# Expert rows padded to 64 instead of 128 in a one-core decoder layer: 32 whole and 4 split tiles in place of 39

## The chip, the cores and the metric

The kernel runs on one core of a Trainium2 chip. The metric is the device time of one execution in microseconds (us); lower is better. The reference's outputs are float32; most matmuls work on pairs of float16 parts (a high part and the remainder), three products for each product of the reference.

## The reference, cut to what matters

One decoder layer on x of shape (8, 256, 256): causal self-attention with 16 heads, a cross-attention of three iterations with a GRU, and a feed-forward with a shared expert and 8 routed experts, of which each token takes two. After each of the three there is a residual and a layer norm. The change touches only the third:

```python
router_probs = softmax(einsum('bsd,de->bse', x, gate_w) + gate_b)
expert_values, expert_indices = top_k(router_probs, k=2)
expert_values = expert_values / (sum(expert_values, axis=-1, keepdims=True) + 1e-09)
h = gelu(einsum('bsd,edi->bsei', x, ew1) + eb1)
all_outputs = einsum('bsei,eid->bsed', h, ew2) + eb2
moe_out = einsum('bse,bsed->bsd', weights_E, all_outputs)
return x + _mlp(x, sh_w1, sh_b1, sh_w2, sh_b2) + moe_out
```

There are T = 2048 tokens, D = 256, I = 1024, E = 8 experts. The kernel computes only the two chosen experts of each token, so 4096 (token, expert) rows.

## The kernel before, in words

**Stages.** Attention takes about the first 0.4 of the span, the cross-attention runs to about 585 us, the shared expert and the routing to about 647 us, the routed experts to about 877 us, and the combine with the last norm to the end. All five engines run programs written out by hand; every dependence is a semaphore.

**Shared expert and routing (about 585 to 647 us).** `ffn_tensor` runs 24 of 32 steps m of the shared expert: `up(m)` is six matmuls of 512 columns, `down(m - 2)` twelve of 256. Between them, listed in `beside`, are the small matmuls of the routing. `ffn_vector` runs `choose_experts`, `count_tokens`, `weigh_choices`, `place_rows`, `part_choices`, `name_rows` and `name_tiles`: some fifty small VectorE operations that depend on one another through the semaphore `r_line`. They count the rows of each expert, give each expert a whole number of 128-row tiles (`tiles`, `ends`, `first`), and give each row its slot. `rows_of(n)` on TensorE (L1955, in steps 16 to 19) turns slots into token numbers; it waits for `part_choices(n)` (L2113, L2117, L2120). The results are `dst` (128 x NTILE, the token row of each place of each tile, or a dummy row for an empty place) and `tile_e` (the expert of each tile). The constant TILES_KNOWN is the value of `r_line` when `tile_e` is ready. GpSimd subtracts the float16 part of each hidden chunk (`hidden_low`, L1839) and issues the gathers.

**Tiles.** NTILE = 2T/128 + E - 1 = 39 tiles of 128 rows. This is the number that always suffices, whatever the router chooses. For every tile i, with double buffers u = i % 2:

1. GpSimd gathers 128 token rows of `rows_x` into `xg` (`gather`, L1769), in its loop in `experts_pool`.
2. TensorE transposes them (`turn`, L1875, two float32 transposes), ScalarE and VectorE split them into `xgT` (L2348, L2392).
3. Up (L2257): for each of 8 chunks k of the hidden dimension, six matmuls of 128 columns. The expert's weight `e1[:, e, ch, h, k]` is the stationary side, `xgT` streams. Three products for each of two halves of D; the weight part h = 0 is used twice in a row, h = 1 once, so there are four different weights for a chunk. The expert number is a register value, so the weight's address is worked out on TensorE's sequencer.
4. VectorE adds the bias (`biased`, L2408), ScalarE applies gelu and casts (`front`, L2354, L2360), VectorE takes the remainder (`hidden_low`, L2413): the hidden parts `he`.
5. Down (L2265, L2266): for each k, `he[u][0][:, k]` is the stationary side and both parts of `e2[:, e, k]` stream (512 columns), then `he[u][1][:, k]` with 256 columns. The stationary side has a fixed address, the streamed one is worked out at run time. The tile's rows come out as PSUM partitions.
6. VectorE adds both halves and the bias (`back`, L2424, L2427) into `yo`, ScalarE scales each row by its router weight (`weigh`, L2366), and GpSimd adds it to `back_y` in DRAM by an indirect DMA (`scatter`, L2229). Each scatter waits for the one before to have landed.

**Order.** TensorE's pass i is `turn(i + 3)`, then `tile_pair(i + 2, .., i, ..)`: the up of tile i + 2 with the down of tile i, interleaved three up matmuls to one down matmul. The first two ups run alone; the last two downs run alone too, each behind one `up(MF + ..)` of the rest of the shared expert. After them come steps MF + 2 to MS of the shared expert, `add_sums` (L2306) and `last_downs`. Expert numbers are loaded into registers 16 at a time (`experts_from`), in passes 14 and 30. ScalarE's pass is `turned(i + 3)`, `weigh(i - 1)`, `front(i + 2)`; `front(i)` waits, before its cast L2360, for D_mm of tile i - 2. VectorE's is `turned(i + 3)`, `biased(i + 2)`, `back(i)`, `hidden_low(i + 2)`.

**Combine.** SyncE waits for all scatters, then loads `back_y` in 8 chunks (`combine_load`, L2463). VectorE takes the statistics (L2494), GpSimd the reciprocal roots, ScalarE and VectorE normalise, SyncE stores (L2476).

Of the kernel before, what the change touches and what calls it, by code (L numbers as in the profile page):

```python
# [34 lines left out]
def decoder_layer(nc, a, out):  # L35
# [17 lines left out]
    NTILE = 2 * T // P + E - 1  # L53
# [3 lines left out]
    with top:  # L57
# [17 lines left out]
        dst = sb(top, "dst", [P, NTILE], I32)  # L75
# [13 lines left out]
        ramp_i = sb(top, "ramp_i", [P, NTILE], I32)  # L89
# [17 lines left out]
        tile_e = sb(top, "tile_e", [P, NTILE], I32)  # L107
# [8 lines left out]
        def constants_pool():  # L116
# [14 lines left out]
            PO.iota(ramp_i[:, :], pattern=[[1, NTILE]], base=0, channel_multiplier=0).then_inc(const_fill, 1)  # L131
# [944 lines left out]
        n_back, n_sum, n_stat, n_rstd, n_norm = (sem(k) for k in ("n_back", "n_sum", "n_stat", "n_rstd", "n_norm"))  # L1076
        NSTAT = 2 * TG + 1
# [6 lines left out]
        NUMBERED = 46  # L1084
# [16 lines left out]
        def norm_sum(g):  # L1101
# [3 lines left out]
                             rows, ALU.add).then_inc(n_sum, 1)  # L1105
            VE.wait_ge(n_sum, g + 1)
            for t in range(TG):
                VE.bn_stats(st2[g % 2][:, t, :], xs[:, g * TG + t, :]).then_inc(n_stat, 1)
            VE.wait_ge(n_stat, NSTAT * g + TG)
# [4 lines left out]
            VE.wait_ge(n_stat, NSTAT * g + 2 * TG)  # L1114
# [567 lines left out]
        with ExitStack() as c:  # L1682
# [22 lines left out]
            def route(*shape):  # L1705
# [13 lines left out]
            cmp1, up8 = route(E, NT), route(E, E)  # L1719
            s1, s2, m2, p2, r0, r1 = (route(NT) for _ in range(6))  # L1720
            slot, top_w = route(2, NT), route(NT, 2)
            total, tiles, ends, first = (route(E) for _ in range(4))
            te_f, ramp, cnt = route(NTILE), route(NTILE), route(1)
            HALF = NT // 2
            behind, places, turn_at = route(1), route(P), route(NT)
# [4 lines left out]
            ramps = reused[:, 0:P + 2 * NT + 1].bitcast(I32)  # L1730
            meant = part(reused, 0, HALF * NTILE, F16).rearrange("p (t n) -> p t n", n=NTILE)
            cmp2 = reused[:, 0:NTILE * E].rearrange("p (t e) -> p t e", e=E)
# [7 lines left out]
            picked = mask[:, 5 * NTILE:6 * NTILE]  # L1740
            ROUND = 1.5 * 2.0 ** 23
# [13 lines left out]
                sem(k) for k in ("U_mm", "U_bias", "U_gelu", "U_hi", "U_lo", "D_mm", "D_out"))  # L1755
            gathered = [sem(f"gathered{q}") for q in range(NT // 2)]
# [7 lines left out]
            NAMED, TILES_KNOWN = NUMBERED + 6, NUMBERED + 11  # L1764
# [53 lines left out]
            def number_constants():  # L1818
# [4 lines left out]
                    (0, NT), (NT, P), (NT + P, NT), (2 * NT + P, 1)))  # L1823
                PO.iota(turns, pattern=[[P, NT]], base=0, channel_multiplier=0).then_inc(made, 1)
# [193 lines left out]
            PARTED = 34  # L2018

            def choose_experts():  # L2020

# [197 lines left out]
            def experts_pool():  # L2219


                def scatter(i):
# [4 lines left out]
                    if i >= 1:  # L2227
                        PO.wait_ge(rows_out[(i - 1) % 2], 16 * ((i - 1) // 2 + 1))
# [347 lines left out]
```

## Time and profile before

| what | us |
|---|---|
| time of the kernel, median of 3 runs | 908.75 |
| lowest of the 3 runs | 908.33 |
| highest of the 3 runs | 1269.37 |
| span of the profiled execution, first to last instruction | 905.5 |
| TensorE busy in the span | 876.6 (97%) |
| VectorE busy | 648.3 (72%) |
| ScalarE busy | 557.3 (62%) |
| GpSimd busy | 365.5 (40%) |

For the profiled execution itself only the span is given, no device time of its own beside it. The 1269.37 us run is an outlier; the two others agree within 0.05%. PE is TensorE's matmuls, PEld its weight loads (they overlap), DVE is VectorE, ACT ScalarE, POOL GpSimd, SP SyncE. Ends of matmuls are modelled, so starts are what to read. L12 is line 12 of the kernel.

### The profile page before, as it was taken

What the parts mean: (1) busy time and instruction counts of PE and PEld (TensorE: products, weight loads), DVE (VectorE), ACT (ScalarE), POOL (GpSimd) and SP (SyncE); (2) the same over time, 40 slices, a digit from 0 to 9 for tenths busy, and PEclk for the clock granted to TensorE, in tenths of its full rate; (3) what the DMA queues carried; (4) which work ended last, traced back from release to release, by engine and by line L of the source; (5) the groups of instructions that cost most, each with busy time, mean ns of one, the idle gap of its engine ahead of it and who ended that gap; (6) DMA issues with size and microseconds to landing.
All of it is one profiled execution on the core that took longest, in us unless ns stands there. A gap on an engine that the chain in (4) does not pass through costs nothing. (4 is left out here: it accounts for less than half of the span.)

```text
span 905.5 us, 23841 instructions
## 1 busy us (share of the span) xinstructions
PE 876.6 (97%) x8190; PEld 669.9 (74%) x8190; DVE 648.3 (72%) x1839; ACT 557.3 (62%) x1347; POOL 365.5 (40%) x492
## 2 busy tenths in 40 slices
PE   5999999999999999999999999999999999999996
PEld 4777777777777777776767676676788888888864
DVE  5667787867676777667878786869677766776655
ACT  6778776767666677656575755545455555554555
POOL 2333433333333465325444442354534444444433
PEclk9999999999999999999999999999999999999998
DMA  9742434242423241230000000099443332333226
GB/s 320 195 141 96 163 107 151 94 142 93 140 76 125 95 150 49 9 94 2 1 1 2 1 1 1 32 356 409 135 107 49 49 49 44 49 49 48 43 30 192
DMA packets 61584, 88.09 MB, mean 97 GB/s; under 512 B 17279, under 2 KB 46527, under 8 KB 61343
## 3 DMA queue, kind: packets, MB, share of 16 engines
q1 hardware_dynamic: 53439, 75.52, 25.3%
q0 software_dynamic: 7488, 10.27, 7.3%
q8 instruction: 72, 1.18, 0.6%
q10 hardware_dynamic: 544, 0.79, 0.3%
q14 instruction: 41, 0.34, 0.1%
HBM read 56.00 MB, written 30.56 MB: 96 GB/s over the span
## 5 line engine op out<-in xcount | busy, mean ns | idle before, releaser
L2257 PE MATMUL ps<-slots,e 128*128 128x128 f16 x1872 | 189.9, 219 | 2.2 <-DVE xs L2424 2.2
L669 POOL TENSOR_SCALAR prob<-prob,rden 128x128 f32<-128x128 f32 (+1 forms) x256 | 110.7, 448 | 200.9 <-DVE rden L958 200.9
L2257 PEld LDWEIGHTS ps<-slots,e 128*128 x1872 | 152.4, 97 | 35.4 <-issue 5.1
L855 ACT ACTIVATE prob<-prob,nmx 128x128 f32<-128x128 f32 (+1 forms) x256 | 114.1, 450 | 40.8 <-DVE nmx L951 37.9
L2265 PE MATMUL ps<-e,xT 128*128 x312 | 117.3, 378 | 0.0
L2354 ACT ACTIVATE slots<-slots 128x512 f32<-128x512 f32 x78 | 49.2, 631 | 107.0 <-DVE slots L2408 107.0
L31 PE MATMUL ps<-xT,wqkv 128*128 128x256 f16 x768 | 96.1, 275 | 0.4 <-DVE wqkv L938 0.4
L31 PEld LDWEIGHTS ps<-xT,wqkv 128*128 128x128 f16 x768 | 70.4, 98 | 29.6 <-issue 21.7
L2266 PE MATMUL ps<-e,xT 128*128 x312 | 85.1, 273 | 0.0
L1769 POOL DMA_INDIRECT xg<-rows_x,dst x39 | 40.9, 1049 | 106.5 <-DVE mask L2397 103.2
L951 DVE CUSTOM_DVE_ANT_0 prob<-ps,mask 128x128 f32<-128x128 f32 (+1 forms) x256 | 75.9, 353 | 3.9 <-PE ps L749 3.9
L2413 DVE TENSOR_TENSOR xT<-slots,xT 128x1024 f16<-128x1024 f32 x39 | 47.8, 1225 | 39.9 <-ACT xT L2360 39.9
L2229 POOL DMA_INDIRECT back_y<-xs,dst x39 | 62.6, 1606 | 29.0 <-DMA back_y<-xs,dst 12.2
L2408 DVE SCALAR_TENSOR_TENSOR slots<-ps,b1e 128x512 f32<-128x512 f32 x78 | 53.8, 692 | 26.5 <-PE ps L2257 26.3
L965 DVE COPY pT<-ps 128x384 f32<-128x384 f32 x64 | 35.6, 556 | 40.8 <-PE ps L720 40.5
L971 DVE TENSOR_TENSOR oT<-ps,oT 128x256 f16<-128x256 f32 x64 | 27.2, 425 | 46.4 <-ACT oT L879 45.9
L749 PE MATMUL ps<-qk 64*128 64x128 f32 (+1 forms) x512 | 59.3, 350 | 0.7 <-ACT qk L865 0.7
L31 PE MATMUL ps<-an,wqkv 120*128 120x256 f16 x432 | 59.0, 272 | 1.0 <-POOL an L1502 1.0
L614 DVE SCALAR_TENSOR_TENSOR parted<-piece,parted 128x256 f16<-128x256 f32 x144 | 57.1, 421 | 0.0
L759 PE MATMUL ps<-pT,v 128*64 128x128 f32 x768 | 56.1, 281 | 0.7 <-DVE pT L965 0.7
L872 ACT COPY pT<-ps 128x384 f32<-128x384 f32 x64 | 30.6, 478 | 41.5 <-PE ps L720 40.1
L720 PE MATMUL ps<-ident,prob 128*128 128x128 f32 x384 | 52.7, 273 | 2.4 <-DVE oT L971 2.0
(275 smaller groups left out, 1939.0 us busy)
## 6 DMA issues: line engine op xcount, KB each, us to landing
halves<-parted SPq DMA_DIRECT2D x36, 512.0 KB, 2.9
piece<-in_L_ffn_ew SPq DMA_DIRECT2D x32, 512.0 KB, 4.5
e<-halves SPq DMA_DIRECT2D x16, 1024.0 KB, 15.4
piece<-in_L_ffn_sh_w SPq DMA_DIRECT2D x4, 512.0 KB, 9.4
sw<-halves SPq DMA_DIRECT2D x4, 512.0 KB, 6.3
rows_x<-xs SPq DMA_DIRECT2D x4, 512.0 KB, 7.7
xs<-back_y SPq DMA_DIRECT2D x8, 256.0 KB, 5.0
out<-xs SPq DMA_DIRECT2D x8, 256.0 KB, 2.1
```

The source lines that it names most:

```text
L31: mm = pe.matmul(out, w, x, start=first and n == 0, stop=last and n == len(products) - 1, **kw)
L614: VE.scalar_tensor_tensor(share(piece_part(q, 1)), share(like_part(q)), WS, share(piece_part(q, 0)), ALU.mult, ALU.subtract).then_inc(p_lo, 1)
L669: PO.tensor_scalar(prob[m % 3][:, h, r], prob[m % 3][:, h, r], rden[m % 2][:, h, t:t + 1], 1.0, ALU.mult, ALU.mult).then_inc(normed, 1)
L749: mm = PE.matmul(ps[:, 2 + h, query_tile(t)], qk[m % 2][r, 0, t * P:t * P + P], qk[m % 2][r, 1, 0:(t + 1) * P], start=True, stop=True)
L759: mm = PE.matmul(ps[r, 4 + t, 384:512], v_sb[m // 2 % 2][:, key, m % 2, r], pT[:, h, at:at + P], start=key == 0, stop=key == t, skip_group ...
L855: SC.activation(p, p, ACT.Exp, bias=nmx[u][:, h, t:t + 1], scale=-1.0, accum_out=den[u][:, h, t:t + 1]).then_inc(exped, 1)
L951: VE.tensor_tensor_reduce(prob[m % 3][:, h, r], ps[:, 2 + h, r], mask[:, r], -1.0, HIGHEST, ALU.add, ALU.min, nmx[m % 2][:, h, t:t + 1]).t ...
L2229: PO.indirect_dma_start(back_y, bass.IndirectOffsetOnAxis(ap=dst[:, i:i + 1], axis=0), yo[i % 2], None, compute_op=ALU.add).then_inc(rows_ ...
L2257: yield PE.matmul(ps[:, 2 * u + q, (k % 4) * P:(k % 4) * P + P], w[ch][h], xgT[u][j][:, ch, :], start=n == 0, stop=n == 3 * DC - 1)
L2265: yield PE.matmul(ps[:, 4 + u, :], he[u][0][:, k, :], w, start=k == 0, stop=False, skip_group_check=True)
L2266: yield PE.matmul(ps[:, 4 + u, 0:D], he[u][1][:, k, :], w[:, 0:D], start=False, stop=k == IC - 1, skip_group_check=True)
L2408: VE.scalar_tensor_tensor(z, ps[:, 2 * u + q, :].rearrange("p (k t) -> p k t", k=4), 1 / WS, bias, ALU.mult, ALU.add).then_inc(U_bias, 1)
```

## The change

Each expert gets a whole number of 64-row halves instead of 128-row tiles. An expert with an odd number of halves has a single half left over; at most 8 experts do, and two such halves share a split tile. So 32 whole tiles (FULL) and 4 split tiles suffice always. `tile_e` has 40 names: one for each whole tile, two for each split one.

- `place_rows` counts whole tiles and single halves apart (`parts`, 256 comparisons in place of 128), works out `paired` and `onward`, and moves the rows of single halves: seven more VectorE operations and several longer ones. `name_tiles` has five more. `name_halves`, new, makes two lists for the scatters of each split tile: rows of the other half point to the dummy rows. It stands after the second tile in VectorE's program.
- Up of a split tile: for each chunk and each of the two experts six matmuls of 64 columns.
- Down of a split tile (`split_down`): the weight is now the stationary side and the hidden half streams with 64 columns, so the result comes out transposed. VectorE copies it (`split_out`), TensorE turns it back (`split_back`, two float32 transposes), VectorE adds the bias for each half (`split_rows`).
- Order: whole tiles go on in pairs (passes 0 to 29); the ups of tiles 32 and 33 go beside the downs of 30 and 31; from pass 32 on, nothing is interleaved.
- A split tile is scattered twice, the second after the first has landed.
- The sum count `n_sum` is folded into `n_stat`, with no change of order.

The core of the diff:

```diff
-    NTILE = 2 * T // P + E - 1
+    HALF_P = P // 2
+    FULL = 2 * T // P
+    NTILE = FULL + E // 2
+    NAMES = FULL + 2 * (NTILE - FULL)
...
 place_rows:
-                VE.tensor_tensor(cmp1, ps[:, 7, E:2 * E].unsqueeze(2).broadcast_to((P, E, NT)), ...
+                VE.tensor_tensor(cmp1, ps[:, 7, E:2 * E].unsqueeze(2).broadcast_to((P, E, 2 * NT)), ...
+                VE.tensor_tensor(parts[:, 0, :], parts[:, 0, :], parts[:, 1, :], ALU.subtract)
+                VE.tensor_scalar(paired, parts[:, 1, :], float(P), None, ALU.mult)
+                VE.tensor_tensor(w0, rank, paired.unsqueeze(1).broadcast_to((P, NT, E)), ALU.is_ge)
+                VE.tensor_scalar(onward, ends[:, 1, :], -float(P), float(HALF_P * (UNITS - 1)), ALU.mult, ALU.add)
+                VE.scalar_tensor_tensor(onward, first[:, 0, :], -float(HALF_P), onward, ALU.mult, ALU.add)
+                VE.tensor_tensor(w0, w0, onward.unsqueeze(1).broadcast_to((P, NT, E)), ALU.mult)
+                VE.tensor_tensor(bf, bf, w0, ALU.add)
...
 scatter:
+                    for m in range(2):
+                        at = NTILE + 2 * (i - FULL) + m
+                        if m == 1:
+                            PO.wait_ge(rows_out[i % 2], rows_gone(i) - 16)
+                        PO.indirect_dma_start(back_y, bass.IndirectOffsetOnAxis(ap=dst[:, at:at + 1], axis=0),
+                                              yo[i % 2], None, compute_op=ALU.add).then_inc(rows_out[i % 2], 16)
...
+                def up_chunk(i, experts, k):
+                    u, q, wide = i % 2, k // 4, P // len(experts)
+                    for m, e in enumerate(experts):
+                        w = [[e1[:, bass.ds(e, 1), ch, h, k * P:k * P + P].squeeze(1) for h in range(2)]
+                             for ch in range(DC)]
+                        at = k % 4 * P + m * wide
+                        for n, (ch, (h, j)) in enumerate(itertools.product(range(DC), HILO)):
+                            yield PE.matmul(ps[:, 2 * u + q, at:at + wide], w[ch][h],
+                                            xgT[u][j][:, ch, m * wide:(m + 1) * wide], start=n == 0, stop=n == 3 * DC - 1)
...
+                def split_down(i, experts):
+                    u = i % 2
+                    by_half = e2[:, :, :, :, :].rearrange("p e (a b) i n -> p (e a) b i n", a=2)
+                    down_ready(i)
+                    for k in range(IC):
+                        for c, (m, e) in itertools.product(range(DC), enumerate(experts)):
+                            rows, at = slice(m * HALF_P, (m + 1) * HALF_P), c * P + m * HALF_P
+                            w = [by_half[:, bass.ds(e * 2 + k // 4, 1), k % 4, h, c * P:c * P + P].squeeze(1) for h in range(2)]
+                            for n, (h, j) in enumerate(HILO):
+                                mm = PE.matmul(ps[:, 4 + u, at:at + HALF_P], w[h], he[u][j][:, k, rows],
+                                               start=k == 0 and at == 0 and n == 0, stop=k == IC - 1 and n == 2,
+                                               skip_group_check=True)
+                    mm.then_inc(D_mm, 1)
...
 TensorE, pass i:
+                    if i < FULL:
+                        tile_pair(i + 2, i, names)
                     else:
-                        up(MF + i - (NTILE - 2))
-                        tile_pair(None, None, i, expert[i])
+                        if i + 2 < NTILE:
+                            tile_up(i + 2, names)
+                        else:
+                            up(MF + i - (NTILE - 2))
+                        if i > FULL:
+                            split_back(i - 1)
+                        split_down(i, experts_of(names, i))
                 for m in range(MF + 2, MS):
                     up(m)
+                    if m == MF + 2:
+                        split_back(NTILE - 1)
...
 ScalarE, pass i:
-                    if i >= 1:
+                    if 1 <= i <= FULL:
                         weigh(i - 1)
                     if i + 2 < NTILE:
                         front(i + 2)
                     else:
                         hidden(MF + i - (NTILE - 2))
-                weigh(NTILE - 1)
+                    if i > FULL:
+                        weigh(i - 1)
                 for m in range(MF + 2, MS):
                     hidden(m)
+                    if m == MF + 2:
+                        weigh(NTILE - 1)
...
 VectorE, pass i:
+                    if i < FULL:
+                        back(i, names[i])
+                    if i > FULL:
+                        split_rows(i - 1, experts_of(names, i - 1))
+                    if i >= FULL:
+                        split_out(i)
                     if i + 2 < NTILE:
                         hidden_low(i + 2)
```

## Rows read from the trace of the kernel before

**Rows 1.** The page: parts 1 and 5 (busy us, mean ns | idle before)

```profile
PE 876.6 (97%) x8190; PEld 669.9 (74%) x8190; DVE 648.3 (72%) x1839; ACT 557.3 (62%) x1347; POOL 365.5 (40%) x492
...
L2257 PE MATMUL ps<-slots,e 128*128 128x128 f16 x1872 | 189.9, 219 | 2.2 <-DVE xs L2424 2.2
```

**Rows 2.** Windows: 676 to 856 us; PE, PEld, DVE, ACT, POOL, clock, DMA, GB/s

```profile
676.00:856.00 180.00, 177.81 (x2079) 150.25 (x2077) 124.15 (x252) 94.91 (x159) 80.90 (x63) 1.00 0.31 49
```

**Rows 3.** Timeline of PE: the transposes of tiles 7 and 38

```profile
680.75 0.38 PE L1875 MATMUL ps<-ident,xg 128*128 128x128 f32 x2
...
858.28 0.38 PE L1875 MATMUL ps<-ident,xg 128*128 128x128 f32 x2
```

**Rows 4.** The chain that ended last: the lone up of tile 1

```profile
654.14 4.03 PE ps L2257 x48
```

**Rows 5.** Lines L2257 and L2265: register operations on TensorE's sequencer (ns min/median/max)

```profile
L2257 PEldq FUSED_REGOPS  x1248: 46/46/46, 648.7 to 869.0; - x179
...
L2265 PEldq ALU_OP  x312: 32/32/42, 658.7 to 874.3; - x156
```

**Rows 6.** Timeline of PE: shared ups around the lone downs

```profile
869.52 1.46 PE L31 MATMUL ps<-xT,sw 128*128 128x512 f16 x6
...
877.31 1.46 PE L31 MATMUL ps<-xT,sw 128*128 128x512 f16 x6
```

**Rows 7.** Timeline: weight loads of the first rows_of (39 columns each)

```profile
625.96 0.27 PEld L1955 LDWEIGHTS ps<-slots 128*128 128x128 f16 x8 [1.21 <-DVE slots L2120]
```

**Rows 8.** Timeline from the last scatters to the last matmuls

```profile
877.75 1.55 POOL L2229 DMA_INDIRECT back_y<-xs,dst  x1 [2.92 <-DMA back_y<-xs,dst]
...
882.30 1.55 POOL L2229 DMA_INDIRECT back_y<-xs,dst  x1 [3.00 <-DMA back_y<-xs,dst]
...
885.96 3.99 SPq L2463 DMA_DIRECT2D xs<-back_y  x8
...
891.63 1.90 PE L2306 MATMUL ps<-xs,routes 128*128 128x256 f32 x8
...
893.37 4.09 PE L31 MATMUL ps<-sw,slots 128*128 128x256 f16 x36
...
898.37 0.76 DVE L2494 BATCH_NORM_STATS2 routes<-ps 128x6 f32<-128x256 f32 x2
```

**Rows 9.** Windows: the clock (1.00 is 2.4 GHz) in two stretches

```profile
901.00:903.00 2.00, 0.00 (x0) 0.00 (x0) 1.26 (x3) 0.78 (x2) 0.00 (x0) 0.50 0.77 258
654.00:658.00 4.00, 4.00 (x50) 3.24 (x47) 2.38 (x5) 1.79 (x3) 0.26 (x1) 1.00 0.72 238
```

**Rows 10.** Timeline of PE at the kernel's start: the same matmuls twice

```profile
10.49 2.62 PE L31 MATMUL ps<-xT,wqkv 128*128 128x256 f16 x12 [0.43 <-DVE wqkv L938]
...
14.72 1.49 PE L31 MATMUL ps<-xT,wqkv 128*128 128x256 f16 x12
```

**Rows 11.** Timeline of the routing, 617 to 647 us

```profile
617.78 0.29 DVE L2078 TENSOR_REDUCE routes<-routes 128x8 f32<-128x128 f32 x1
...
618.62 1.09 DVE L2085 TENSOR_TENSOR routes<-routes 128x8 f32<-128x8 f32 x1
...
625.97 0.37 PE L1955 MATMUL ps<-slots 128*128 128x39 f16 x8 [0.72 <-DVE slots L2120]
...
638.85 0.18 DVE L2150 CAST tile_e<-routes 128x39 int32<-128x39 f32 x1
...
646.93 0.38 PE L1875 MATMUL ps<-ident,xg 128*128 128x128 f32 x2
```

**Rows 12.** Timeline: VectorE's part of turned(3) and TensorE's turn(4)

```profile
662.72 0.42 DVE L2392 TENSOR_TENSOR slots<-ps,slots 128x256 f16<-128x256 f32 x1
...
663.88 0.38 PE L1875 MATMUL ps<-ident,xg 128*128 128x128 f32 x2
```

**Rows 13.** Groups of instructions by line, 676 to 856 us: cast and scale

```profile
L2360 ACT CAST xT<-slots 128x1024 f16<-128x1024 f32 x32 | 33.5, 1045 | 1.0
...
L2366 ACT ACTIVATE xs<-xs,mask 128x256 f32<-128x256 f32 x32 | 16.3, 509 | 0.0
```

More of the change, by code:

```diff
@@ L1740, in decoder_layer @@
             picked = mask[:, 5 * NTILE:6 * NTILE]
+            apart, own = mask[:, 6 * NTILE:7 * NTILE - FULL], mask[:, 7 * NTILE:7 * NTILE + 1]
+            sides = [mask[:, 7 * NTILE + 1 + m:7 * NTILE + 2 + m] for m in range(2)]
+            split_to = mask[:, 8 * NTILE:8 * NTILE + NAMES - FULL].rearrange("p (t m) -> p t m", m=2)
             ROUND = 1.5 * 2.0 ** 23
@@ L2294, in tile_pair @@
                                 last_down = mm
-                        if up is not None and k % 4 == 3:
+                        if k % 4 == 3:
                             last_up.then_inc(U_mm, 1)
-                    if down is not None:
-                        last_down.then_inc(D_mm, 1)
+                    last_down.then_inc(D_mm, 1)
                 def add_sums():
@@ L2407, in biased @@
                             VE.wait_ge(U_lo, i)
-                        VE.scalar_tensor_tensor(z, ps[:, 2 * u + q, :].rearrange("p (k t) -> p k t", k=4), 1 / WS,
-                                                bias, ALU.mult, ALU.add).then_inc(U_bias, 1)
+                        for m, e in enumerate(experts):
+                            rows = slice(m * wide, (m + 1) * wide)
+                            bias = b1e[:, bass.ds(e, 1), 4 * q:4 * q + 4].squeeze(1).unsqueeze(2).broadcast_to((P, 4, wide))
+                            done = VE.scalar_tensor_tensor(z[:, :, rows], up[:, :, rows], 1 / WS, bias, ALU.mult, ALU.add)
+                        done.then_inc(U_bias, 1)
                 def hidden_low(i):
@@ L2428, in back, with split_out, split_rows @@
                                             ALU.add).then_inc(D_out, 1)
+                def split_out(i):
+                    VE.wait_ge(D_mm, i + 1)
+                    if i >= FULL + 2:
+                        VE.wait_ge(Y_mm, i - FULL - 1)
+                    VE.tensor_copy(yT[:, i % 2, :], ps[:, 4 + i % 2, 0:D]).then_inc(D_out, 1)
+                def split_rows(i, experts):
+                    u = i % 2
+                    VE.wait_ge(Y_mm, i - FULL + 1)
+                    VE.wait_ge(rows_out[u], rows_gone(i - 2))
+                    for m, e in enumerate(experts):
+                        rows = slice(m * HALF_P, (m + 1) * HALF_P)
+                        done = VE.scalar_tensor_tensor(yo[u][rows, :], ps[rows, 4 + u, D:2 * D], 1 / WS,
+                                                       b2e[rows, bass.ds(e, 1), :].squeeze(1), ALU.mult, ALU.add)
+                    done.then_inc(D_out, 1)
                 VE.wait_ge(r_line, TILES_KNOWN)
-                expert = experts_from(mybir.EngineType.DVE, 0)
+                names = experts_from(mybir.EngineType.DVE, 0)
                 turned(0)
@@ L2435, in experts_vector @@
                 for i in range(2):
-                    biased(i, expert[i])
+                    biased(i, names)
                     hidden_low(i)
@@ L2440, in experts_vector @@
                         shared_base(2)
+                name_halves()
                 for i in range(NTILE):
-                    if (i + 2) % LOADED == 0 and i + 2 < NTILE:
-                        expert += experts_from(mybir.EngineType.DVE, i + 2)
+                    if (i + 2) % LOADED == 0 and i + 2 < NAMES:
+                        names += experts_from(mybir.EngineType.DVE, i + 2)
                     if i + 3 < NTILE:
```

240 lines of the change are left out of this document (156 added, 84 removed).

## The prediction

> **What bounds the kernel now.** The page comes first. TensorE is busy 97% of the span, no other engine over 72%, and the costliest group is L2257, the experts' up projections with 1,872 matmuls [rows 1]. Next the windows: between 676 and 856 us TensorE is busy 177.81 of 180 us, VectorE 124, ScalarE 95, GpSimd 81, at granted clock 1.00 [rows 2]. So in the loop over expert tiles the time of a tile is TensorE's. The timeline gives it: the transposes (L1875) that open a pass start at 680.75 and, 31 passes later, at 858.28 [rows 3], 5.73 us each. Two of the 31 passes load expert names into registers and take about 1.2 us more; the others take 5.65 us.
>
> What fills 5.65 us? The transposes take 0.38 [rows 3]. The rest is 48 up matmuls of 128 columns, 8 down matmuls of 512 and 8 of 256: 12,288 columns in some 5.27 us, 0.43 ns a column, which is the 2.4 GHz level. A paired pass is bound by columns. But the first up projection runs alone, and there 48 matmuls (6,144 columns) take 4.03 us [rows 4], 84 ns each and not the 55 of their columns. Every expert weight has an address made at run time: TensorE's sequencer issued 1,248 FUSED_REGOPS of 46 ns for L2257 and 312 ALU_OPs of 32 ns for L2265 [rows 5]: 32 and 8 per tile. 4.03 us over 32 addresses is 126 ns per address, each with its loads and the one or two matmuls that use it. So there are two bounds: columns (0.43 ns each) and weight addresses (126 ns each). A paired pass needs 32 x 0.126 = 4.03 us plus 8 ALU_OPs for addresses, below 5.27, and the wide down matmuls hide them. That margin is what the change uses up.
>
> **The change, part by part.** All sums are against the span of 905.5 us; the median of the timed runs, 908.75, is 3.25 us above it, and I add that at the end.
>
> *What goes.* 39 tiles become 36. Paired passes of two whole tiles fall from 37 to 30: 7 x 5.65 = 39.6 us. The two passes that hold a down projection alone (869.52 to 877.31, 3.9 us each, of which 1.3 is a shared up of six 512-column matmuls [rows 6]) lose 2 x 2.6 = 5.2 us. Together 44.8.
>
> *A split up projection.* Its matmuls have 64 columns, twice as many, for two experts: 64 addresses instead of 32. The columns would cost 6,144 x 0.43 = 2.6 us, the addresses 64 x 0.126 = 8.06 us. The trace has no 64-column matmul with a run-time address. The bounds are 27 ns for each of the 96 (64 columns; the loads of eight matmuls of 39 columns at fixed addresses took 0.27 us [rows 7], and with 0.10 for the last the other seven are (0.27 - 0.10)/7 = 25 ns apart) and 84 ns (the lone up, with the same form of address and also two addresses to three matmuls [rows 4]). I take 84 ns: the split only doubles the number of such groups. Tiles 32 and 33 go up beside whole downs (which add 8 ALU_OPs, between 0 and 0.15 us each, since (5.27 - 4.03)/8 = 0.15; I take 0.11): 8.06 + 0.9 + 0.38 = 9.35 us, twice, 18.7. Tiles 34 and 35 go up alone: 8.06 + 0.38 and 8.06, 16.5.
>
> *A split down projection.* It no longer streams the weight (512 columns, one ALU_OP for two matmuls); it loads it as the stationary side: 8 chunks x 2 column halves x 2 experts x 2 parts = 64 addresses. Its index is `e * 2 + k // 4`, one or two register operations more; going from an ALU_OP of one to a FUSED_REGOPS (46 against 32 ns, [rows 5]) an operation costs little, say 7 ns. Bounds: 2.6 us (columns) to 10.9 us (the extra ones as an instruction of their own, 170 ns per address); I take 64 x 0.134 = 8.6 us. Four of them, none beside anything: 34.4. Three transposes back inside the loop: 3 x 0.4 = 1.2.
>
> Loop: 18.7 + 16.5 + 34.4 + 1.2 - 44.8 = +26.0 us, for three tiles fewer.
>
> *The scatters.* Each split tile adds to back_y twice, the second waiting for the first to land. Before, where one scatter waits for the last, they start 4.55 us apart (877.75, 882.30) and the last lands at 885.96, 3.66 us on, when the loads of the combine start [rows 8]. In the whole tiles this has room (one per 5.65). Now look at ScalarE's program order: `weigh(i - 1)` stands behind `front(i + 2)` for split tiles, and `front(35)` waits for D_mm of tile 33. So tile 32 is scaled only after the down of tile 33 ends; call that T. Then come the cast (1.05) and the scale (0.5) [rows 13]: the first of eight half scatters starts at T + 1.7 and the eighth lands at T + 1.7 + 7 x 4.55 + 3.66 = T + 37.2. TensorE's last two passes take 2 x (1.3 + 0.4 + 8.6) = 20.6, so the loads of the combine start 16.6 us after the last down, where before it was 8.5 (877.47 to 885.96). Tail: +8.1 us. The shared ups and downs that follow (877.5 to 891.6, some 14 us [rows 6, 8]) no longer cover it: the first chunk landed about 5.2 us after its load began (885.96, VectorE and TensorE go on at 891.2 and 891.63), so TensorE idles about 16.6 + 5.2 - 14.7 = 7 us before `add_sums` (L2306 [rows 8]).
>
> *The clock.* Before, TensorE's last matmuls end at 897.46 [rows 8], and over 901 to 903 the granted clock is 0.50, its 1.2 GHz level [rows 9]. So after 7 us idle add_sums and the first of the last downs start at that level: 1.74 us (891.63 to 893.37) becomes 3.5, and at the kernel's start 12 matmuls of 256 columns took 2.62 us, and 1.49 a little later [rows 10]. Some 2.9 us more (1.74 and, for 12 matmuls, 1.13), 0.9 of it covered (the last downs end at 897.46, VectorE takes their sums at 898.37 [rows 8]): +2.0.
>
> *The head.* place_rows runs on VectorE while TensorE waits: its first routing matmul (L1955, 625.97) sits idle 0.72 us for L2120 [rows 11], so what is added there is added to the end. Seven more small operations (128 elements 0.29 us [rows 11], 8 or 16 elements about 0.17, and 0.03 between), 1.7 us, and longer ones (256 for 128 elements, a ramp of 116 for 39), 0.5: +2.2. It can be 1 us more where one is held up, as L2085 was (8 elements, 1.09 us [rows 11]). name_tiles' added 1.6 us cost nothing: the names are known at 639.0, and TensorE loads them one shared pass (some 2.6 us) before turn(0) at 646.93 [rows 11], near 644. name_halves (7 operations, 1.3 us) stands on VectorE ahead of turned(3), done at 663.14 while TensorE wants it at 663.88 [rows 12]: 1.3 - 0.7 = +0.7 (0 to 1.5). VectorE's split halves of the bias and of the output, and the iotas, lie beside a TensorE that is now slower: nothing.
>
> Sum: +26.0 + 8.1 + 2.0 + 2.2 + 0.7 = +39.0. Span 944.5; with 3.25, 947.8 us.
>
> **Rivals.**
> *A, columns set the split tiles.* If half-width matmuls cost their columns and the address work is hidden, a split tile costs 2.6 up and 2.6 down. For it: the 39-column loads [rows 7] and the paired passes. Against: [rows 4], a lone up at 84 ns with column time of 55. To T the time from pass 30 is then 2 x 5.65 + 3.0 + 2.6 + 2.6 + 0.4 + 2.6 = 22.5 us, plus 37.2 for the scatters, 59.7; before it is 7 x 5.65 + 7.8 + 8.5 = 55.9. So +3.9, head 2.9, clock 2.0: 917.5, not slower by the measure used here. It decides if an address costs under about 60 ns. The Trainium skill, "TensorE: Matmul & The Clock Gate", section "Back-to-back issue gap", gives this price: a warm matmul's gap is its columns over 2.4 GHz plus 2.5 ns, never under about 25 ns. The same section has 81 ns for a stream of loads and matmuls at 128 columns, near the 84 here, but without the address operations.
> *B, the added index operations are instructions of their own*: 10.9 us a down, of which two lie before T and the last two are hidden by the scatters: +4.6, 952.
> *C, half scatters are cheaper or overlap* (only 64 rows carry values). For it: the 3.66 us of landing is most of the 4.55. Against: each still moves 128 rows. Then the tail is about +3 and the clock does not fall: 941.
> *D, the clock falls in the split passes*, with their narrow matmuls. At 1.2 GHz the mixed passes are bound by columns again (10.6 us, +1.3 each), and the shared matmuls behind double and outlast the scatters: +10, 958. Against: over the lone up, 654 to 658, the granted clock stayed at 1.00 [rows 9].
>
> **How the numbers follow.** Forecast 0.52, A 0.10, B 0.13, C 0.17, D 0.08. The time is the forecast's, 947. The range 928 to 960 leaves out A and a little above D. A measurement of this kernel tells about 2% (18 us) from no change: slower by more, over 927, holds the forecast, B, C and D, 0.88; within it A and a small remainder, 0.10; faster by over 2% would need a scatter chain that vanishes too, 0.02.
>
> **What would show it.** In the profile after: the paired whole passes unchanged at 5.65 us; about 16 us between the starts of the last lone passes; FUSED_REGOPS of 64 per split up and 64 per split down, and split matmuls 80 to 90 ns apart; eight scatters about 4.5 us apart after the down of tile 33, the loads of the combine waiting for the last, and TensorE idle before add_sums at clock 0.5; the first L1955 waiting near 3 us. Split matmuls under 40 ns apart would prove the forecast wrong (A); scatters under 3 us apart would prove its tail wrong.

## The result and the profile after

| | before | after |
|---|---|---|
| median of the timed runs, us | 908.76 | 944.07 |
| span of the profiled execution, us | 905.5 | 941.0 |
| TensorE busy in the span, us | 876.6 | 906.5 |
| mean granted clock | 0.997 | 0.973 |

The change makes the kernel slower: the ratio of the times is 1.0403, with an interval of 1.0389 to 1.0417. The forecast was 947.8 us by the sum (stated as 947), in a range of 928 to 960. The page of the kernel after, parts 1, 2 (the clock) and 5, answers to [rows 1]:

```profile
PE 906.5 (96%) x8512; PEld 694.3 (74%) x8512; DVE 642.3 (68%) x1846; ACT 548.7 (58%) x1332; POOL 364.6 (39%) x493
...
PEclk9999999999999999999999999999999999996578
...
L2343 PE MATMUL ps<-slots,e 128*128 128x128 f16 (+1 forms) x1920 | 189.1, 218 | 2.1 <-DVE xs L2560 1.1
```

TensorE is busy 30 us longer although three tiles are gone, and its clock falls late in the span. L2343 is now the up, L2351 and L2352 the whole tiles' down, L2366 the split down, L1904 the transposes that open a pass, L2375 the transposes back. The timeline of TensorE, from the pass with tile 30's down on, answers to [rows 3] and [rows 6]:

```profile
831.12 0.38 PE L1904 MATMUL ps<-ident,xg 128*128 128x128 f32 x2
...
841.55 0.39 PE L1904 MATMUL ps<-ident,xg 128*128 128x128 f32 x2
...
851.51 0.40 PE L1904 MATMUL ps<-ident,xg 128*128 128x128 f32 x2
...
877.29 0.67 PE L2375 MATMUL ps<-ident,routes 128*128 128x128 f32 x2
877.75 8.35 PE L2366 MATMUL ps<-xT,e 128*128 128x64 f16 x96
886.10 2.72 PE L31 MATMUL ps<-xT,sw 128*128 128x512 f16 x6
888.61 0.63 PE L2375 MATMUL ps<-ident,routes 128*128 128x128 f32 x2
```

The two mixed passes (a split up beside a whole down) take 10.43 and 9.96 us. From 851.5 to 886.1 there are two split ups and two split downs, 8.4 to 8.6 us each. The chain that ended last shows all four; these are its rows for the first up and the first down (start, us, what; a "PE" piece counts its matmuls):

```profile
851.90 3.71 PE ps L2343 x45
855.71 4.59 PE ps L2343 x51
860.31 3.93 PE ps L2366 x45
864.30 4.62 PE ps L2366 x51
```

96 matmuls in 8.6 us are 90 ns each. The register operations by line, answering to [rows 5], give what they wait for. 1,280 for the ups are 32 for each of 32 whole tiles and 64 for each of 4 split ones; the 256 of the split downs are 64 each:

```profile
L2343 PEldq FUSED_REGOPS  x1280: 46/46/46, 650.4 to 877.1; - x183
...
L2366 PEldq FUSED_REGOPS  x256: 46/46/60, 860.2 to 905.7; - x128
```

The scatters and the loads of the combine, from the timeline (first, second and last of eight half scatters), answer to [rows 8]:

```profile
887.92 2.00 POOL L2312 DMA_INDIRECT back_y<-xs,dst  x1 [31.03 <-ACT xs L2495]
...
892.59 1.55 POOL L2312 DMA_INDIRECT back_y<-xs,dst  x1 [2.67 <-DMA back_y<-xs,dst]
...
918.32 1.55 POOL L2312 DMA_INDIRECT back_y<-xs,dst  x1 [2.49 <-DMA back_y<-xs,dst]
...
922.25 3.95 SPq L2624 DMA_DIRECT2D xs<-back_y  x8
...
927.76 3.36 PE L2428 MATMUL ps<-xs,routes 128*128 128x256 f32 x8 [5.13 <-DMA xs<-back_y]
```

GpSimd (POOL) had waited 31 us for ScalarE's scaling and starts 1.8 us after the down of tile 33 has ended at 886.10. Then each scatter waits for the one before, on average 4.34 us from start to start, and TensorE idles 5.13 us. The head, answering to [rows 11]: the first routing matmul waits 3.06 us where it had waited 0.72.

```profile
628.06 0.37 PE L1984 MATMUL ps<-slots 128*128 128x36 f16 x8 [3.06 <-DVE slots L2164]
```

The span is 35.5 us longer. In three stretches: up to the transposes of tile 33, which stood at 828.86 and stand at 831.12, +2.26; from there to the loads of the combine, 57.10 us before (to 885.96) and 91.13 after (to 922.25), +34.03; from the loads to the end, 19.54 before and 18.75 after, -0.79.

### The profile page after: what moved, and what is told of

It is laid out like the page before. It is cut to its first block and busy times, and to the rows that moved or that the text cites. A ratio compares the mean times of both kernels' runs of the same rounds, so it can differ in the third digit from the quotient of the medians.

```text
span 941.0 us, 24674 instructions
## 1 busy us (share of the span) xinstructions
PE 906.5 (96%) x8512; PEld 694.3 (74%) x8512; DVE 642.3 (68%) x1846; ACT 548.7 (58%) x1332; POOL 364.6 (39%) x493
## 5 line engine op out<-in xcount | busy, mean ns | idle before, releaser
L2343 PE MATMUL ps<-slots,e 128*128 128x128 f16 (+1 forms) x1920 | 189.1, 218 | 2.1 <-DVE xs L2560 1.1
L2343 PEld LDWEIGHTS ps<-slots,e 128*128 x1920 | 152.7, 98 | 35.7 <-issue 5.1
L2483 ACT ACTIVATE slots<-slots 128x512 f32<-128x512 f32 x72 | 45.3, 630 | 115.9 <-DVE slots L2544 110.6
L2351 PE MATMUL ps<-e,xT 128*128 x256 | 96.8, 378 | 0.1
L31 PEld LDWEIGHTS ps<-xT,wqkv 128*128 128x128 f16 x768 | 70.4, 98 | 29.6 <-issue 21.8
L2544 DVE SCALAR_TENSOR_TENSOR slots<-ps,b1e 128x512 f32<-128x512 f32 (+1 forms) x80 | 50.0, 636 | 39.7 <-PE ps L2343 39.4
L1788 POOL DMA_INDIRECT xg<-rows_x,dst x36 | 37.1, 1032 | 97.3 <-DVE mask L2529 81.1
L2352 PE MATMUL ps<-e,xT 128*128 x256 | 69.8, 273 | 0.0
L2549 DVE TENSOR_TENSOR xT<-slots,xT 128x1024 f16<-128x1024 f32 x36 | 44.1, 1225 | 36.4 <-ACT xT L2489 36.4
L975 DVE COPY pT<-ps 128x384 f32<-128x384 f32 x64 | 35.5, 555 | 40.9 <-PE ps L730 40.6
L2303 POOL DMA_INDIRECT back_y<-xs,dst x32 | 51.1, 1598 | 24.1 <-ACT xs L2495 14.6
L2016 ACT ACTIVATE slots<-ps,b1s 128x512 f32<-128x512 f32 x32 | 22.0, 687 | 57.6 <-PE ps L31 47.5
```

Of the source, the lines that this page charges most:

```text
L31: mm = pe.matmul(out, w, x, start=first and n == 0, stop=last and n == len(products) - 1, **kw)
L2303: PO.indirect_dma_start(back_y, bass.IndirectOffsetOnAxis(ap=dst[:, i:i + 1], axis=0), yo[i % 2], None, compute_op=ALU.add).then_inc(rows_ ...
L2343: yield PE.matmul(ps[:, 2 * u + q, at:at + wide], w[ch][h], xgT[u][j][:, ch, m * wide:(m + 1) * wide], start=n == 0, stop=n == 3 * DC - 1)
L2351: yield PE.matmul(ps[:, 4 + u, :], he[u][0][:, k, :], w, start=k == 0, stop=False, skip_group_check=True)
L2352: yield PE.matmul(ps[:, 4 + u, 0:D], he[u][1][:, k, :], w[:, 0:D], start=False, stop=k == IC - 1, skip_group_check=True)
```

## The experiments

**Is it the addresses?** The first run takes the address work away and leaves every matmul; it leaves out the right choice of experts in the split tiles.

```diff
-                        w = [[e1[:, bass.ds(e, 1), ch, h, ...
+                        w = [[e1[:, (bass.ds(e, 1) if wide == P else slice(m, m + 1)), ch, h, ...
-  w = [by_half[:, bass.ds(e * 2 + k // 4, 1), k % 4, h, ...
+  w = [by_half[:, 2 * m + k // 4, k % 4, h, ...
```

> The changed kernel, with the expert weights of the four split tiles taken at fixed addresses (experts 0 and 1) instead of addresses worked out at run time; the split tiles so compute with the wrong experts, everything else is as in the changed kernel. Theory 1 (the price of a split tile is its 64 + 64 run-time weight addresses): no register operations are left between the split matmuls, they start 27 to 30 ns apart, a lone split up or down takes 2.6 to 2.9 us instead of 8.6, the two mixed passes fall from about 10.2 to 5.7 us, the clock stays at 1.00, and, the eight scatters after the down of tile 33 being as they were, the time falls by some 32 us to about 912. Rival (the price lies in the 64-column matmuls and their 128x128 weight loads themselves, or in the low clock): they stay 73 to 89 ns apart and the time stays near 944.

Measured: 912.3 us, ratio to the kernel before 1.0054 (1.0029 to 1.0079). The chain, over the first three of the same four lone passes:

```profile
843.23 2.80 PE ps L2343 x96
846.03 2.80 PE ps L2366 x96
848.83 2.80 PE ps L2343 x96
```

96 matmuls with 96 weight loads take 2.80 us in place of 8.4 to 8.6, 29.2 ns from one to the next. The mixed passes took 5.62 us. So of the 35 us that the change costs, 32 hang on run-time addresses. This is also rival A made true (it was priced at 917.5 us), and it shows that even then 36 tiles do not win: the time stays at 1.0054 of the kernel before. The tail and the head take back what the passes save.

**Is it the 64 columns?** The kernel before, with every up matmul cut in two.

```diff
+                        for m in range(2):
+                            at = (k % 4) * P + m * 64
-                        yield PE.matmul(ps[:, 2 * u + q, (k % 4) * P:(k % 4) * P + P], w[ch][h], xgT[u][j][:, ch, :], ...
+                            yield PE.matmul(ps[:, 2 * u + q, at:at + 64], w[ch][h], xgT[u][j][:, ch, m * 64:m * 64 + 64], ...
```

> The kernel before, with every up matmul of 128 columns issued as two of 64 columns with the same weight one after the other: 96 up matmuls and loads a tile, still 32 run-time addresses. Theory 1 (addresses): a pass keeps its 5.65 us or gains little (the columns are the same; at most 2.5 ns a matmul, 0.1 us), the lone up stays near 4.0. Rival (a half-width matmul with its load costs 80 ns or more by itself): a pass takes 8.5 us or more and the whole time rises by over 100 us.

Measured: 914.4 us, one time, beside 908.2; 1,872 more matmuls in all for 6 us. A paired pass takes 5.8 us instead of 5.65. In it six matmuls of 64 columns stand where three of 128 stood, and L2267 follows 0.17 us later (two of the timeline's rows):

```profile
661.06 0.34 PE L2259 MATMUL ps<-slots,e 128*128 128x64 f16 x6
661.23 0.38 PE L2267 MATMUL ps<-e,xT 128*128 x1
```

The second run in this pair was meant to double the addresses too.

> The same 96 up matmuls of 64 columns, but in the order of the change: first six for one half of the rows, then six for the other, each half with its own run-time addresses, 64 a tile. Theory 1: every pass takes about 10 us as the two mixed passes of the changed kernel, the lone ups about 8, and the time rises by 37 x 4.3 + 2 x 4 = 167 us to about 1075. Rival (64-column matmuls are dear whatever their addresses): the same time as the run with 32 addresses.

Measured: 913.1 us. The experiment missed its aim: the trace counts the same 1,248 FUSED_REGOPS as before. Two slices with the same expert register share one computed address here.

```profile
L2259 PEldq FUSED_REGOPS  x1248: 46/46/46, 650.1 to 874.8; - x179
```

It says again that 64 columns are cheap, in the order of the change too (passes of 5.7 to 5.8 us), and nothing of addresses. So it serves as the control of the next run, which has the same matmuls in the same order. That one loads the expert numbers of eight tiles a second time, into other registers, and uses them for the second half of the rows.

```diff
+                        if i + 2 == 16:
+                            _, again = nc.values_load_multi_w_load_instructions(tile_e[0:1, 16:24], ...
-                        tile_pair(i + 2, expert[i + 2], i, expert[i])
+                        tile_pair(i + 2, expert[i + 2], i, expert[i], again[i - 14] if 16 <= i + 2 < 24 else None)
```

> The kernel before, with the up matmuls of tiles 16 to 23 alone split in two halves of 64 columns, first six for one half of the rows, then six for the other, the second half with the expert number from a second load into other registers (the same experts, the same result), so that 64 addresses are worked out for each of these eight tiles. The earlier run had kept 32 addresses a tile in both orders, because equal numbers share their addresses, and 64 columns alone cost little. Theory 1 (126 ns per address): the eight passes take 9.9 to 10.4 us instead of 5.65, as passes 30 and 31 of the changed kernel, and the time rises by some 36 us to 945. Rival (the dear thing in the changed kernel's split passes is something else, such as two experts in one PSUM bank): they take 5.8 us, as in the run with 64 columns and 32 addresses, and the time stays below 912.

Measured: 941.1 us, one time, beside 908.2. The passes are 9.83 to 9.96 us long (openings of three of them), and the line of the eight tiles has 64 operations for each:

```profile
748.54 0.39 PE L1875 MATMUL ps<-ident,xg 128*128 128x128 f32 x2
758.48 0.39 PE L1875 MATMUL ps<-ident,xg 128*128 128x128 f32 x2
768.31 0.39 PE L1875 MATMUL ps<-ident,xg 128*128 128x128 f32 x2
```

```profile
L2260 PEldq FUSED_REGOPS  x512: 46/46/46, 739.0 to 817.5; - x171
```

This is the price measured by itself, in the old kernel and with the old work: 9.9 - 0.38 us for 64 addresses and 8 ALU_OPs, 135 ns an address if an ALU_OP costs the 0.11 us that the prediction took.

**Is it the clock?** In the kernel after the granted clock falls in the lone split passes; with a dense matmul put into each chunk of them it does not.

```diff
+                def filler():
+                    PE.matmul(ps[:, 6, :], s1c[0][:, 0, 0:P], xT[:, NG - 1, 0, 0, :], start=True, stop=True)
```

> The changed kernel, with one more matmul of 512 columns at fixed addresses, whose product nobody reads, at the head of each of the 8 chunks of the lone ups of tiles 34 and 35 and of the downs of tiles 32 and 33: 32 matmuls, 6.8 us of columns at 2.4 GHz. Theory 1 (address-bound, with room for columns, and the granted clock of 0.50 adding to it): they hide between the addresses, the clock stays at 1.00, a lone split pass falls from 8.6 us to about 7.3 as the downs of 34 and 35 (7.2 us, at a clock of 1.00 for part of the time) and the time falls by about 5 us to 939 although work was added. Rival a (the clock does not matter to an address-bound pass): they hide, and the time stays at 944. Rival b (no room): it rises by 7 us to 951.

Measured: 944.6 us, ratio 1.0409 (1.0391 to 1.0426), the same as the change alone; the expected gain of 5 us did not come. The windows over the four lone passes, of the kernel after and then of this run (PE, PEld, DVE, ACT, POOL, clock, DMA, GB/s):

```profile
856.00:886.00 30.00, 29.80 (x339) 25.67 (x338) 5.53 (x13) 3.56 (x5) 0.89 (x1) 0.50 0.05 7
```

```profile
856.00:886.00 30.00, 29.88 (x366) 24.39 (x364) 5.64 (x13) 3.56 (x5) 1.02 (x1) 1.00 0.05 7
```

32 matmuls were added, of which the trace has 27 more in these 30 us, at twice the clock, and nothing moved: rival a. Here an address-bound pass has room for columns and does not feel the clock. A pass of wide matmuls does. The shared up behind these passes, six matmuls of 512 columns, runs 2.51 us in the kernel after (886.10 to 888.61, above) at a granted clock of 0.50, and 1.29 us in this run at 1.00:

```profile
886.44 1.46 PE L31 MATMUL ps<-xT,sw 128*128 128x512 f16 x6
887.73 0.38 PE L2381 MATMUL ps<-ident,routes 128*128 128x128 f32 x2
```

These 1.2 us change nothing in the time, since the chain of scatters ends later than TensorE's work in both kernels.

Why are the split downs of 34 and 35 shorter (889.04 to 896.14, 7.1 us)? The windows of their line (PE and PEld, with counts; clock) begin to show it:

```profile
889.00:890.00 1.00, 0.96 (x24) 0.96 (x24) 0.69 0.00 0
890.00:891.00 1.00, 1.00 (x22) 0.81 (x17) 1.00 0.65 36
891.00:892.00 1.00, 1.00 (x14) 0.78 (x12) 1.00 0.68 112
```

The first 46 matmuls start in 2 us, the others 13 or 14 a microsecond. A shared up of six wide matmuls stands ahead of them, and the register operations of this down (first and last start at the end of the row) begin during it:

```profile
L2366 PEldq FUSED_REGOPS  x64: 46/46/60, 886.7 to 895.9; - x64
```

The 64 addresses take 9.2 us from 886.7 on, no less than elsewhere, but the first matmul comes only at 889.04: TensorE's sequencer works ahead while the wide matmuls run. The kernel before shows the same in the lone up of tile 0, which stands behind wide shared matmuls:

```profile
L2257 PEldq FUSED_REGOPS  x30: 46/46/46, 648.7 to 652.4; - x30
...
649.99 2.99 PE L2257 MATMUL ps<-slots,e 128*128 128x128 f16 x48
```

Its 48 matmuls take 2.99 us, where those of tile 1 take 4.03 [rows 4]. No run varied the lead.

**The tail.** Two runs on the scatters. First ScalarE's order:

```diff
-                    if 1 <= i <= FULL:
+                    if i >= 1:
                         weigh(i - 1)
...
-                    if i > FULL:
-                        weigh(i - 1)
```

> The changed kernel, with ScalarE's scaling of a split tile put back ahead of the gelu and cast of the tile two further on, as for whole tiles. Theory 1 (the scatters of tile 32 start only after the down of tile 33 because ScalarE's order holds them): the first half scatter starts at about 879 instead of 888, the last of the eight at about 915 (tiles 34 and 35 are then ready only just in time), the loads of the combine begin 3 to 4 us earlier, TensorE idles under 2 us before add_sums instead of 5.1 and may keep its clock, and the time falls by 4 to 6 us to about 939. Rival (the tail is set by something else): no change, 944.

Measured: 940.0 us, ratio 1.0368 (1.0342 to 1.0394) against 1.0403 for the change: 3 to 4 us better. The first half scatter starts at 880.29, as expected, and the loads at 917.66, 4.6 us earlier (3 to 4 were expected). TensorE waits 2.29 us before add_sums, and the clock does not hold: add_sums takes 3.22 us, at a granted clock of 0.50 over 924 to 926 (from the timeline):

```profile
880.29 1.55 POOL L2312 DMA_INDIRECT back_y<-xs,dst  x1 [23.07 <-ACT xs L2495]
...
923.33 3.22 PE L2428 MATMUL ps<-xs,routes 128*128 128x256 f32 x8 [2.29 <-DMA xs<-back_y]
```

Then the number of scatters: `for m in range(1)` instead of 2 in `scatter`, and the counts to match.

> The changed kernel, with only the first of the two scatters of each split tile (the rows of its second expert are left out of the result). Theory 1 (eight scatters one after the other set the tail): four scatters, each waiting for its tile, the last landing at about 914; TensorE's shared matmuls end near 922.6 and then go on without idling; the time falls by about 5 us to 939. Rival (the scatters are hidden anyway): no change.

Measured: 939.4 us, ratio 1.0355 (1.0331 to 1.0379). Each scatter now waits for its tile, the loads begin at 914.56, and add_sums follows the shared matmuls without a wait:

```profile
910.76 1.55 POOL L2312 DMA_INDIRECT back_y<-xs,dst  x1 [8.14 <-ACT xs L2495]
...
914.56 3.94 SPq L2624 DMA_DIRECT2D xs<-back_y  x8
...
922.26 1.89 PE L2428 MATMUL ps<-xs,routes 128*128 128x256 f32 x8
```

So the chain of scatters, as the change has it, is worth some 4 to 5 us over one that is hidden. This is not the price of the low clock: in this run too the first two shared ups take 2.5 us each instead of 1.3, and now TensorE's work sets the end. No run joined the filler with it.

**The orientation of the down.** If addresses are dear and columns cheap, the split down should stream its weights as before, at twice the columns.

```diff
-                def down_chunk(i, e, k):
+                def down_chunk(i, experts, k):
+                    for m, e in enumerate(experts):
+                        w = e2[:, bass.ds(e, 1), k, :, :].squeeze(1).rearrange("p i n -> p (i n)")
+                        bank = down_place(i, m)
-                    yield PE.matmul(ps[:, 4 + u, :], he[u][0][:, k, :], w, ...
+                        yield PE.matmul(ps[:, bank, :], he[u][0][:, k, :], w, ...
...
-                    if i < FULL:
+                    if i + 2 < NTILE:
                         tile_pair(i + 2, i, names)
```

`down_place` is bank 4 or 5 for the first expert and 6, 7, 0, 1 for the second of tiles 32 to 35; VectorE reads 64 rows from each.

> The changed kernel, with the down projections of split tiles in the old orientation: the hidden parts stationary at fixed addresses for all 128 rows, the weights of each of the two experts streamed (512 and 256 columns, 12,288 columns a tile instead of 6,144), each expert in a PSUM bank of its own of which only its rows are read; no transposes back; downs 32 and 33 interleaved with ups 34 and 35; the scaling ahead as for whole tiles. Two scatters stay. It computes the reference. Theory 1 (weight addresses are the price, columns are cheap): passes 32 and 33 take some 10.6 us in place of 17.2, the lone downs of 34 and 35 take 5.3 instead of 7.2, the loads of the combine begin some 22 us earlier, and the time falls to about 922, in spite of twice the columns in the downs. Rival (columns count): the downs take longer than before and the time does not fall below 940.

Measured: 924.7 us, ratio 1.0181 (1.0164 to 1.0198). Passes 32 and 33 take 21.8 us together, and the lone down 5.2 behind its shared up. The timeline of TensorE:

```profile
856.48 0.39 PE L1904 MATMUL ps<-ident,xg 128*128 128x128 f32 x2
...
878.30 1.46 PE L31 MATMUL ps<-xT,sw 128*128 128x512 f16 x6
...
884.79 1.46 PE L31 MATMUL ps<-xT,sw 128*128 128x512 f16 x6
```

19 us of the 35 are gone, with 24,576 columns more (four tiles, 6,144 each). Not all of this is the orientation's: the run also interleaves two downs with ups and scales ahead, and the latter alone was worth 3 to 4 us in the run above. Counted from the transposes of tile 33, the loads of the combine begin 20.8 us earlier than in the kernel after (22 were expected), and TensorE still waits 6.51 us for them: the eight half scatters still set the end. The run beats the change and not the kernel before.

**The second tile's neighbour.** The call of `name_halves` moved from behind tile 1 to the head of pass 24 on VectorE.

> The changed kernel, with name_halves moved on VectorE from behind the second tile to the head of pass 24. Theory 1 (there VectorE has some 1.6 us to spare in each pass, and behind the second tile it has not): the delay of turn(4) against the kernel before falls from 2.2 us to about 1, and the time falls by 1.2 us, to 942.9. Rival (the 1.2 us between turn(3) and turn(4) come from something else, for example the longer routing): no change, 944.1.

Measured: 944.5 us in runs from 942.0 to 950.9, ratio 1.0421 (1.0395 to 1.0447): the expected gain is not there, and the time does not resolve 1.2 us. The trace does. In the kernel after, the transposes of tile 3 come 0.97 us later than before and those of tile 4 2.16 us later, with a wait; in this run both come some 2.66 us late, without one. First the kernel after, then this run:

```profile
666.04 0.41 PE L1904 MATMUL ps<-ident,xg 128*128 128x128 f32 x2 [0.99 <-issue]
```

```profile
660.75 0.41 PE L1904 MATMUL ps<-ident,xg 128*128 128x128 f32 x2
666.55 0.40 PE L1904 MATMUL ps<-ident,xg 128*128 128x128 f32 x2
```

So name_halves costs 1.2 us where it stood. That this run is late already at tile 3 has another reason. Behind TensorE's wait of 3.06 us in the routing, twelve shared matmuls took 2.46 us instead of 1.31, and the granted clock (the third figure from the end) is down there. The profiled run of the kernel after has the same wait without that fall. The window, busy times as above:

```profile
628.80:631.20 2.40, 2.40 (x16) 1.72 (x14) 2.37 (x5) 0.00 (x0) 0.00 (x0) 0.51 1.02 410
```

The last run joins it with the streamed downs.

> The changed kernel with streamed downs for split tiles (as in streamed_downs, 924.7 us) and with name_halves at the head of pass 24: the best of the versions so far for 36 tiles. Theory 1: the two gains add up, 923.5 us, still 1.7% slower than the kernel before, since the ups of four split tiles still cost 64 addresses each and eight scatters still follow one another. Rival (36 tiles win once the split downs are streamed): at or under 908.

Measured: 920.9 us beside 906.7 for the kernel before, ratio 1.0170 (1.0146 to 1.0194), not to be told from the 1.0181 of the streamed downs alone: that the gains add up is not shown. No version with 36 tiles that computes the whole reference came below the kernel before.

## Why the prediction was right, and where it was off

**The bound of a split tile: right.** 64 addresses for an up and 64 for a down, whatever the columns. Priced were 126 ns (up) and 134 ns (down); the lone passes of 8.4 to 8.6 us are 131 to 134 for both. With the address work taken away the same matmuls start 29 ns apart, and with it doubled in the old kernel, where the control at single addresses has 5.8 us, the passes take 9.9 us: that is the proof. Rival A fell with the first of these runs. The Trainium skill ("TensorE: Matmul & The Clock Gate", section "Back-to-back issue gap") gives a warm matmul by itself its columns over 2.4 GHz plus 2.5 ns, from which 29.2 ns is an estimate for 64 columns. At fixed addresses the trace has just that, 2.80 us for 96, weight loads included; with run-time addresses it has 90 ns. One reading was incomplete: [rows 4] is the lone up of tile 1, and the first lone up, of tile 0, took 2.99 us, below the 4.03 that was called the bound of 32 addresses, because its addresses were begun ahead.

**The loop: right in sum, in part by luck.** The stretch to the loads of the combine came to +34.03 against 26.0 + 8.1 = 34.1, because three errors of 1 to 2 us cancel. From the transposes of tile 33 to T the forecast has 18.7 + 16.5 + 17.2 + 0.4 = 52.8 us and the trace 54.98, 2.2 too little. Of this 1.7 are the mixed passes, put at 9.35 us and measured at 10.43 and 9.96: address operations and wide down matmuls overlap less than taken, and the first of the two also loads expert names. Before, the pass that loads them takes 6.85 us (828.86 to 835.71) and not 5.65, so that the stretch before was put 1.2 us too short as well (55.9 against 57.10). The third error is the 1.05 us of the scatters below. The downs of tiles 34 and 35 were put at 8.6 and took 7.1; this gave nothing, since the scatters end later.

**The tail: right.** First scatter at T + 1.8 (T + 1.7), steps of 4.34 (4.55), loads at T + 36.2 (T + 37.2). Rival C, cheaper half scatters, fell: a half scatter takes nearly as long as a whole one. What the tail is worth in time was less than its 8.1 us: with half of the scatters the loads begin 7.7 us earlier, but the shared matmuls, which end at 922.26, then set the end, and 4.6 us are won.

**The clock: two steps failed.** First, "after 7 us idle add_sums and the first of the last downs start at that level ... +2.0". TensorE idled 5.13 us, and add_sums took 3.36 us instead of 1.74, at a granted clock of 0.50 over 928 to 930; the last downs did not slow down (the clock is 1.00 over 931 to 935). But the stretch from the loads to the end became 0.79 us shorter. The +2.0 took the path through add_sums to be the one that ends last in both kernels. Before, it is not: VectorE starts on the statistics at 891.20 because it is busy until then with a remainder of the shared expert (L2457, ahead of the statistics in its program), and TensorE starts add_sums at 891.63 behind a shared up, without a wait. Neither waited for the first chunk, as the prediction had read it. The chain that ended last goes through the next of these remainders, at 893.20, and then through VectorE's and GpSimd's statistics. The rows of before:

```profile
890.59 0.69 DVE L2457 TENSOR_TENSOR slots<-slots 128x512 f16<-128x512 f32 x1 [1.91 <-ACT slots L1992]
891.20 1.07 DVE L2494 BATCH_NORM_STATS2 routes<-xs 128x6 f32<-128x256 f32 x3
...
893.20 0.69 DVE slots L2457
```

After, VectorE is nearly through with the shared expert and starts on the statistics 2.65 us behind the loads, instead of 5.24, and the chain goes through add_sums and the last downs:

```profile
924.90 1.49 DVE L2655 BATCH_NORM_STATS2 routes<-xs 128x6 f32<-128x256 f32 x4 [2.78 <-DMA xs<-back_y]
...
931.12 3.94 PE ps L31 x36
```

What VectorE gained made room for what TensorE lost. That the sum of the two is -0.79 and not zero is read from the trace; no run varied it.

Second, rival D was dismissed because the clock stayed at 1.00 over the lone up. It did fall, to 0.50 over 856 to 886, in passes without idle time. Its price was wrong in both parts. The mixed passes ran before the fall, at 1.00. The shared matmuls did run at nearly half speed: the three shared ups take 2.51, 2.24 and 2.54 us instead of 1.29, and with the three pairs of transposes back and the first shared down the loss comes to some 4.7 us. But they did not outlast the scatters: TensorE still stood idle for 5.13 us before add_sums. So neither clock error touched the sign.

**The head: right, a little too dear.** +2.9 forecast, +2.26 measured. The first rows_of waits 2.3 us more, as said, but the four of them then stand 2.81 us apart instead of 3.00 [rows 11 show the first]: VectorE's last operation of `part_choices`, which took 1.43 us each time before (L2120), takes 0.45 in two of the four rounds after (L2164), and TensorE no longer waits for it in the last three. Why it is faster there is not shown. The kernel before also waits 0.72 us for a gather ahead of the transposes of tile 2, which the kernel after does not. Both were put at nothing. So only 0.97 us of the delay are left at tile 3, and name_halves, with 1.2 us and not 0.7, brings it to 2.16.

## What to carry to other kernels

Before cutting tiles smaller to save padding, count what a tile costs that is not columns. Here a weight address made at run time costs about 130 ns on TensorE's sequencer; it was hidden in passes with 5.27 us / 32 = 165 ns of columns per address, and stood bare where the columns per address were cut to a fraction. Turning the product so that the run-time operand streams (one address for two wide matmuls) can be cheaper even at twice the columns, and wide matmuls ahead of an address-bound stretch give the sequencer a lead (seen in two places, varied by no run). And work that was a single indirect scatter per tile, done as two that wait for each other, needs the same count made for its queue at the end of the loop, where nothing follows to hide it.

## What the hardware showed that I had not expected

- The granted clock fell to 0.50 (1.2 GHz) with TensorE busy 29.8 of 30 us by the profile, in passes of narrow matmuls spaced by address work, and stayed at 1.00 when one 512-column matmul per chunk was added. The four lone passes began at 851.51 and 851.64 and ended at 886.10 and 886.44: they took the same time at either clock, while a shared up of six 512-column matmuls took 2.51 us at 0.50 and 1.29 at 1.00.
- TensorE's sequencer worked out addresses up to 2.3 us before the matmul that needs the first of them (886.7 and 889.04), while wide matmuls ran. The down behind them took 7.1 us in place of 8.4 to 8.6, with the same 64 addresses.
- Two slices that use the same expert register share their address operations (1,248 with 96 as with 48 up matmuls a tile); the same number in another register does not.
- Indirect scatters of which half of the rows go to dummy rows landed no sooner: 3.8 us after their issue, the median of both kinds, and 4.34 us from start to start on average where whole ones had 4.55.
